# One transformer layer on one core: five queues in another hand-written order, and the loop over chunks written out

## The reference

```python
x      = layernorm(hidden)
mixed  = silu(causal_conv4(x @ Wqkv.T))            # q, k, v; 4 taps per channel
z      = x @ Wz.T
beta   = sigmoid(x @ Wb.T)
g      = -exp(A_log) * softplus(x @ Wa.T + dt_bias)
for each head, token by token:                      # state S, 128 x 128
    S = exp(g_t) * S
    S = S + k_t (beta_t * (v_t - k_t S))
    o_t = q_t S
y      = rmsnorm(o) * norm_w * silu(z)
x1     = layernorm(y @ Wout.T) + hidden
y2     = shared_expert(x1) + sum over chosen experts of w_e * D_e(relu(G_e x1)^2 * U_e x1)
out    = layernorm(y2) + x1
```

## Time and profile before

| | us |
|---|---|
| median of three runs | 3363.12 |
| the three runs | 3366.53, 3363.12, 3360.05 |
| span of the profiled execution | 3361.6 |
| TensorE busy in it | 3184.6 (95%) |
| VectorE busy | 2731.3 (81%) |
| ScalarE busy | 2411.1 (72%) |
| GpSimd busy | 2147.3 (64%) |

### The profile page before, as it was taken

How to read it: one execution, slowest core, us unless ns; L and a number is a source line. 1 busy time by engine, 2 the same in 40 slices (tenths; PEclk the granted TensorE clock), 3 DMA queues, 4 the chain that set the end, 5 groups by cost and what they waited for, 6 DMA issues and landing times.

```text
span 3361.6 us, 77100 instructions
## 1 busy us (share of the span) xinstructions
PE 3184.6 (95%) x23968; PEld 2828.4 (84%) x23968; DVE 2731.3 (81%) x8720; ACT 2411.1 (72%) x5922; POOL 2147.3 (64%) x5380
## 2 busy tenths in 40 slices
PE   4999999999999999999999999999999999999996
PEld 3888888888888888888888888888888888888885
DVE  4788888888888888888888888888888888888874
ACT  3777777777777777777777777777777777777762
POOL 3766666666666666666666666666666666666660
PEclk8999999999999999999999999999999999999997
DMA  4111111111111111111111111111111111111110
GB/s 182 43 40 38 44 40 35 45 41 38 39 45 35 39 47 38 36 45 38 38 45 41 36 37 46 38 39 47 37 35 45 41 38 42 43 35 39 47 36 11
DMA packets 424113, 144.75 MB, mean 43 GB/s; under 512 B 211168, under 2 KB 421664, under 8 KB 423200
## 3 DMA queue, kind: packets, MB, share of 16 engines
q1 hardware_dynamic: 423712, 139.83, 15.9%
HBM read 93.11 MB, written 46.66 MB: 42 GB/s over the span
## 4 chain that ended last, share of the span: by engine, by line
PE 66%; ACT 14%; DVE 5%; issue 5%; POOL 5%; DMA 4%; SPq 0%; ACTq 0%; DVEq 0%; POOLq 0%
PE bF L474 8%; PE bB L648 6%; PE bQ L547 5%; ACT L850 4%; PE bXT L560 4%; PE bB L733 3%; PE bB L720 3%; PE bS L615 3%; PE bD L630 3%; PE bS L623 3%; PE bF L485 3%; PE bS L607 3%; PE bF L487 3%; PE bD L608 2%; PE bX L570 2%
## 5 line engine op out<-in xcount | busy, mean ns | idle before, releaser
L1151 DVE SCALAR_TENSOR_TENSOR Y<-bF,Cv,Y 128x127 f32<-128x127 f32 (+2 forms) x3072 | 852.2, 339 | 8.3 <-ACT Y L867 3.4
L474 PE MATMUL bF<-XnT,Wqkv 128*128 128x128 f32 x4096 | 530.9, 277 | 0.5 <-ACT XnT L986 0.5
L474 PEld LDWEIGHTS bF<-XnT,Wqkv 128*128 128x128 f32 x4096 | 504.4, 193 | 9.3 <-issue 1.8
L867 ACT ACTIVATE Y<-bF,Cv 128x128 f32<-128x128 f32 x1024 | 383.4, 455 | 102.5 <-PE bF L474 102.5
L937 ACT ACTIVATE XiT<-bXT 128x512 fp32r<-128x512 f32 x384 | 229.0, 596 | 298.0 <-PE bXT L560 293.4
L1590 POOL TENSOR_TENSOR Tp<-Tp 32x64 f32<-32x64 f32 (+2 forms) x768 | 362.1, 472 | 60.2
L1194 DVE TENSOR_TENSOR Qi<-bQ,Cf 128x512 fp32r<-128x512 f32 x384 | 262.8, 684 | 98.1 <-PE bQ L547 97.0
L850 ACT ACT_TABLE_LOAD x257 | 329.7, 1283 | 5.4 <-PEq L1674 0.7
L560 PEld LDWEIGHTS bXT<-Qi,Xi 128*128 128x128 f32 x1536 | 221.8, 191 | 118.0 <-issue 88.8
L560 PE MATMUL bXT<-Qi,Xi 128*128 128x128 f32 x1536 | 298.7, 317 | 14.3 <-DVE Qi L1194 2.5
L1583 POOL TENSOR_TENSOR Tp<-Yb,Tm 32x64 f32<-32x64 f32 (+1 forms) x384 | 276.0, 719 | 30.1
(11 more groups left out here) (234 smaller groups left out, 9269.8 us busy)
## 6 DMA issues: line engine op xcount, KB each, us to landing
DL<-Ln SPq DMA_DIRECT2D x128, 256.0 KB, 2.2
XiT<-DX SPq DMA_DIRECT2D x128, 256.0 KB, 2.8
Xi<-DX SPq DMA_DIRECT2D x128, 256.0 KB, 3.2
DX<-Yb SPq DMA_DIRECT2D x256, 32.0 KB, 1.9
Xf<-x SPq DMA_DIRECT2D x32, 128.0 KB, 3.1
Wqkv<-wqkv SPq DMA_DIRECT2D x4, 1024.0 KB, 17.0
Cb<-DL SPq DMA_DIRECT2D x128, 32.0 KB, 1.9
Xr<-x SPq DMA_DIRECT2D x32, 128.0 KB, 3.3
```

The lines of the kernel that those rows point to most:

```text
L474: last = mm(bank[:, i, :], Wqkv[:, k, c:c + P], XnT[:, k, :], start=(k == 0), stop=(k == KT - 1))
L867: last = op(Y[:, tile, :], bank[:, i, :], ACT.Identity, scale=c[:, TAPS - 1:TAPS], bias=c[:, TAPS:TAPS + 1])
L1151: last = stt(y, bank[:, i, 0:P - shift], Cv[:, g * TILES + tile, n:n + 1], y, ALU.mult, ALU.add)
```

## The change

On each of the five queues the stages of an item are called in another order; no stage is added, removed or changed, and the list for bank bB stays. The loop over chunks becomes a plain loop of the program that writes the kernel, so every chunk is written out. Cut to what is spoken of later (each `if` line belongs to the line under it):

```diff
-        def run(eng, item):
+        def run(item):
...
-            steps = next(n for n in (30, 6, 5, 3, 2, 1) if (chunks - 2) % n == 0)
-            with eng.Fori(0, (chunks - 2) // steps) as i:
-                for k in range(steps):
-                    for g in range(GROUPS):
-                        item((i * steps + k + 1, g), "cafispe")
+            for t in range(1, chunks - 1):
+                for g in range(GROUPS):
+                    item((t, g), "cafispe")
...
                 if "f" in stages:
                     triangle_out(f)
                     blocks_in(f)
+                if g == GROUPS - 1 and "e" in stages:
+                    tokens_out(t - 1)
+                if "f" in stages:
                     inverses_out(f)
                     inverses_in(f)
-                if g == GROUPS - 1 and "e" in stages:
-                    tokens_out(t - 1)
...
                 if invert:
                     invert_q(v, 0, front)
...
-                if state:
-                    ks_qs(w, 1)
...
-                if invert:
-                    invert_xt(v, 0, front)
-                    invert_x(v, 0, front)
                 if e and g == 3:
                     experts(t - 1, "G", 3, a if new else (chunks - 1, GROUPS - 1))
                 if e and g == 2:
                     experts(t - 1, "G", 1, a if new else (chunks - 1, GROUPS - 1))
-                if invert:
-                    invert_q(v, 1)
-                if state:
-                    solve(w, 1)
                 if post:
                     out_proj(u)
                 if invert:
+                    invert_xt(v, 0, front)
+                    invert_x(v, 0, front)
+                if state:
+                    ks_qs(w, 1)
+                if invert:
+                    invert_q(v, 1)
...
+                if state:
+                    solve(w, 1)
+                if invert:
                     invert_xt(v, 1)
                     invert_x(v, 1)
...
+                if c and g == 0:
+                    chunk_front(t + 1, "ba")
+                if state:
+                    out_norm(w)
                 if invert:
                     inverse(v, 2)
...
+                if new:
+                    ended(a)
+                    taps(a, 0, 1)
+                    tails_out(a, 0)
+                    taps(a, 0, 0)
+                if c and g == 0:
+                    chunk_front(t + 1, "norm")
+                if new:
+                    first_tokens(a, 0)
+                if state:
+                    update_o(w, 0)
...
+                if post:
+                    accumulate(u)
+                if e and g == 3:
+                    experts(t - 1, "U", 3)
+                if new:
+                    taps(a, 1, 1)
                 if state:
                     right_side(w, 1)
-                if new:
-                    first_tokens(a, 0)
-                    taps(a, 1, 2)
...
                 if invert:
                     mask_q(v, 1)
-                if new:
-                    taps(a, 1, 1)
```

More of the change, by code:

```diff
@@ L771, in item @@
                 if front:
+                    ktr(f)
                     vtr(f)
+                if state:
+                    solve(w, 0)
+                if e and g == 1:
+                    experts(t - 1, "hT", 0)
+                if front:
+                    parts_t(f)
+                if new:
+                    proj(a, 1, 1)
+                if c and g == 1:
+                    chunk_front(t + 1, "gc")
+                if front:
                     exponents(f)
+                if e and g == 1:
+                    experts(t - 1, "ffn1", 0)
                 if state:
@@ L1090, in item @@
                     experts(t - 1, "ffo", 0)
+                if c and g == 0:
+                    chunk_front(t + 1, "ba")
+                if state:
+                    out_norm(w)
                 if invert:
                     inverse(v, 2)
[L1093 to L1098, removed]
                 if e and g == 0:
                     experts(t - 1, "norm2", 0)
-            run(act, item)
+            run(item)
         @block.vector
@@ L1385, in item @@
                     squares(f)
+                if post:
+                    gated(u)
+                if state:
+                    refined(w)
+                    right_side(w, 0)
+                if c and g == 1:
+                    chunk_front(t + 1, "sp")
+                if e and g == 1:
+                    experts(t - 1, "hn", 0)
+                if front:
+                    products(f)
+                if new:
+                    taps(a, 0, 2)
+                if c and g == 1:
+                    chunk_front(t + 1, "gc")
@@ L1386, in item @@
                 if new:
                     ended(a)
[L1388 to L1395, removed]
+                    taps(a, 0, 1)
+                    tails_out(a, 0)
+                    taps(a, 0, 0)
+                if c and g == 0:
+                    chunk_front(t + 1, "norm")
                 if new:
-                    taps(a, 0, 2)
-                    taps(a, 0, 1)
@@ L1399, in item @@
-                if e and g == 1:
-                    experts(t - 1, "hn", 0)
+                    first_tokens(a, 0)
                 if state:
                     update_o(w, 0)
[L1403 to L1408, removed]
+                if e and g == 1:
+                    experts(t - 1, "shared", 0)
                 if invert:
@@ L1410, in item @@
                     mask_q(v, 0)
-                if c and g == 0:
-                    chunk_front(t + 1, "norm")
+                if new:
+                    taps(a, 1, 2)
+                if state:
+                    update_s(w, 0)
+                if e and g == 2:
+                    experts(t - 1, "U", 1)
+                if post:
+                    accumulate(u)
+                if e and g == 3:
+                    experts(t - 1, "U", 3)
+                if new:
+                    taps(a, 1, 1)
@@ L1448, in item @@
                     experts(t - 1, "norm1", 0)
-                if e and g == 3:
-                    experts(t - 1, "la", 0)
+                if state:
+                    update_o(w, 1)
+                if invert:
+                    mask_q(v, 2)
                 if e and g == 1:
@@ L1468, in item @@
                     experts(t - 1, "ffo", 0)
-                    experts(t - 1, "result", 0)
                 if c and g == 0:
                     chunk_front(t + 1, "ba")
-            run(dve, item)
+                if e and g == 3:
+                    experts(t - 1, "result", 0)
+                if e and g == 1:
+                    experts(t - 1, "route", 0)
+            run(item)
         @block.gpsimd
@@ L1624, in item @@
                     base_inverse(f)
-            run(pool, item)
+            run(item)
 def kernel(**inputs):
```

136 lines of the change are left out of this document (54 added, 82 removed).

## The result

The changed kernel takes 3501.47 us (median of four runs, 3492.74 to 3504.08) against 3362.07: ratio 1.0407, 95% interval [1.0391, 1.0423]. It is 139 us slower; the forecast was 49 us slower, and its range ended at 3470. The sign was right and the size was not.

What follows compares the result with a forecast made beforehand. TensorE, busy 101.67 of 104.60 us, sets the time. Per chunk g0 +0.55, g1 -0.95, g2 and g3 +0.4 each give +0.4, or +1.6 with half the first_tokens collisions; 31 x 1.6 = 49 on 3363: 3412 us, range 3305 to 3470.

Steps and rivals of the forecast that it cites:

- Part 1: TensorE's new order fills its old waits in all four items: a prize of 4.7 us a chunk, 146 us in all.
- part 2: In g2 and g3 out_proj directly behind G waits uncovered for ScalarE's Rl: 0.75 to 0.8 each, net +0.4 us each.
- Part 5: first_tokens on VectorE meets GpSimd's operations in g1, g2 and g3: at most 2.4 us a chunk, half taken, 1.2.
- The first rival: first_tokens wins the race against GpSimd in all items, so collisions cost nothing: 3375 us, chance 0.21.
- Part 3: In g0 VectorE's longer queue makes mask_q 1 late, and SyncE's later loads add waits: item 24.4 us, +0.55.
- The sign that it named: In g0 xt 1 (L559) would wait for VectorE's Qi, with the mask at about 17 us into the item.
- the store's place: In g0 SyncE's DX writes and loads queue behind the result's store: the norm waits 0.6 us for Xf, Xi slightly late.
- Parts 2 and 4: part 2, and for g1 a gain of 1.3 us less about 0.35 for later Xi and As, taken as -0.95.
- The second, that VectorE is not late in g0: Rival: mask_q 1 ends by 14.75 us into g0, which saves 2.2; with no collision 3289 us, chance 0.25.
- The third, all three collisions: Rival: first_tokens is stretched by GpSimd in g1, g2 and g3: +2.8 us a chunk, 3450 us, chance 0.12.

Runs made afterwards that it cites:

- e1: Changed kernel, first_tokens of half 0 taking its second operand from PSUM, the chunk before's part left out: 3402.01 us, ratio 1.0129 to the kernel before.
- e5: Changed kernel with first_tokens of half 0 moved between the taps, where GpSimd is idle, operands still in SBUF: 3407.31 us, ratio 1.0119 to the kernel before.
- e2: Changed kernel with out_proj behind level 0 in g2 and g3, and values ahead of G1's relu on ScalarE: 3460.7 us, ratio 1.0287 to the kernel before.
- e3: Changed kernel with SyncE storing the result behind the DX writes and the XiT and Xi loads, as before: 3500.8 us, ratio 1.0408 to the kernel before.
- e4: Changed kernel with first_tokens' operand in PSUM (chunk before's part left out), out_proj behind level 0 in g2 and g3, store behind loads: 3356.53 us, ratio 0.9991.
- e7: Changed kernel, first_tokens between taps, out_proj behind level 0 and right_side 1, mask_q 1 ahead of taps (1,1) in g2 and g3, store behind loads: 3362.07 us.

## Why the prediction was wrong, point by point

**Part 1** named the right waits: they are gone. What they were worth is another matter, see part 2 below.

**Part 5 is the first step that failed**: "A race of 0.15 us can't be placed by such a count. I take half, 1.2." Measured, by e1 against the changed kernel, it is 2.33 a chunk, nearly the upper bound of 2.4 (e5 gives 2.17). The mechanism was right; the size was not. GpSimd leads by 0.38 in g2 and g3 (1622.97 to 1623.35) and by 0.20 in g1, and in these three items the add is stretched in every steady chunk. Half stood for not knowing: three items that are each won or lost can give 0, 0.75, 0.9, 1.5, 1.65 or 2.4, and the count, which had GpSimd first in all three, pointed to 2.4. This is 35 us of the 90 missing. The first rival (first_tokens wins) falls with it. Not every race is so steady: in g0, which the prediction left out, the same add meets attention in 16 of 28 chunks and is lengthened in 12, and TensorE doesn't wait for it there.

**The clock is the second**: the sum had no term for it. 0.98 a chunk, 30 us. The earlier trace rows show full clock in the steady part before, and I took it as given, but the change puts two waits of 0.7 to 0.8 within 2 us of each other in g2 and g3. Taking either away (e1, e2) leaves no halved clock in these two items; the 0.18 and 0.13 that remain lie in g0, where the changed kernel has 0.18 too. The mean granted clock rises with it in every run, to 0.981 to 0.987 and 0.985 to 0.987. That it falls behind these waits is shown so; that it must fall is not, since it does in some chunks only.

**Part 3** was close. From the item's first product at 1560.79, in the changed kernel (VectorE, then SyncE):

```profile
1564.56 0.54 DVE L1374 TENSOR_SCALAR Yo<-bB,Mv,Ve 128x256 f32<-128x256 f32 x1 [1.68 <-ACT Ve L981]
...
1572.52 0.43 DVE L1265 BATCH_NORM_STATS2 St<-Xf 128x6 f32<-128x256 f32 x1 [0.57 <-DMA Xf<-x]
...
1578.06 0.67 DVE L1196 TENSOR_TENSOR Qi<-bQ,Cf 128x512 fp32r<-128x512 f32 x1
```

```profile
1565.59 0.36 SPq L402 DMA_DIRECT2D out<-Yo  x1
1565.99 1.02 SPq L415 DMA_DIRECT2D DX<-Yb  x2
...
1569.46 0.50 SPq L398 DMA_DIRECT2D Xf<-x  x1
```

The result starts 3.77 in (forecast 3.8), Xf goes out 8.67 in (8.77), the norm waits 0.57 for it (0.6), and mask_q 1 ends at 17.9 (17.8 with that wait). This item takes 24.48 (24.4); the mean is 24.70, since Xi's wait varies up to 2.5. The sign that it named did not come: xt 1 (L559 of level 1) waits for its mask in no steady chunk, though it starts just behind it. TensorE waits ahead of it in this item, for Xi (1.10 a chunk), for S (0.44) and for R (0.35). Of the 0.75 that the prediction gave to the store's place, e3 shows 0.41, and no gain in time. g0's 0.3 and g1's 0.25 over the forecast, 14 us with the rest, and some 10 us in fill and drain and beside the span complete the 90.

**Parts 2 and 4** held as sums, part 2 by luck in g3. With part 5 taken out (e1), g1 is 26.88, -0.71 against before (forecast -0.95), g2 26.07, +0.31 (+0.4), g3 24.88, +0.45 (+0.4). The wait in part 2, 0.75 to 0.8, is 0.78. But part 2 counted a wait that only needs cover, and in g3 cover gains nothing (e2), because solve 1 hangs on out_proj by way of accumulate and R. With all three places mended (e4) the prediction's own terms would make g0 to g3 -0.15, -0.95, -0.4 and -0.4 against before; measured are -0.1, -0.8, -0.2 and +0.5. So the prize of part 1 is nearly there in g1, half there in g2, and absent in g3. There e4 has solve's wait for R, 0.47 a chunk, at the end of this chain of the new VectorE order, which no part named; e7, which takes one step out of the chain, is 0.2 shorter in g3. What holds the rest of g3 up is open.

**The rivals.** The second, that VectorE is not late in g0, falls: the mask ends at 17.9, not 14.75. The third, all three collisions, is the case that occurred: 2.8 a chunk forecast, 3.19 measured at full clock; its 3450 lacked the clock and the rest of g0 and g1.

## What to carry to other kernels

Before an instruction with two SBUF operands on VectorE is moved, look up in the trace what GpSimd does at that time: 0.16 us of work cost 100 us of the kernel, in either order, because an item waited for it. Where several such races are open, forecast the cases that can occur, not their mean, and check in the trace whether one round is like the next: here it was in three items and not in the fourth. Where a new wait comes to stand next to another, leave a term for the clock beside the wait itself: here 30 of the 139 us. And price a move beside the orders of the other queues as they are: out_proj directly behind G cost 189 us in one of these orders and 41 in the other.

## What the runs showed of the hardware

VectorE's add of 128 x 12 elements took 0.16 us by itself, 0.166 to 0.169 in all of 128 cases with one operand in PSUM (e1), and with both in SBUF up to 1.51 (half 1 in the kernel before). Where it met a running minus_l or attention in g1, g2 and g3 of the changed kernel, it ended 0.03 behind that operation (0.92 long in g2, 1.10 in g1), and the operation kept its 1.27. TensorE's granted clock fell to half for 3.41 us behind a stretch of 3.34 us in which it was busy for 1.86; an equal stretch one chunk later left it at full clock, so the stretch alone doesn't decide it, and what else does stays open.
